# Layer 1 attention: keys and queries turned by 32x32 blocks and through memory instead of on TensorE

## The reference

```python
q = (hidden_states @ Wq + bq).reshape(b, n, H, HD)      # H = 32 heads, HD = 128
k = (hidden_states @ Wk + bk).reshape(b, n, H, HD)
v = (hidden_states @ Wv + bv).reshape(b, n, H, HD)
q = rmsnorm(q, gq)
k = rmsnorm(k, gk)
scores = jnp.einsum('bnhd,bmhd->bhnm', q, k) * scale
attn = jax.nn.softmax(scores.astype(jnp.float32), axis=-1)
out = jnp.einsum('bhnm,bmhd->bnhd', attn, v).reshape(b, n, H * HD)
return out @ Wo + bo
...
x = _layernorm(x + _L1_attn_ref(x, ...), axis=-1)
```

## Time and profile before

| | us |
|---|---|
| median of three runs | 3010.38 (3010.3 to 3012.96) |
| the profiled execution | 3012.17 |
| its span, first to last instruction | 3010.1 |
| layer 1's attention in it | about 1151 to 2737 |
| busy in the span: PE, DVE, ACT, POOL | 2884.7, 2234.3, 1590.2, 1955.5 |

### The profile page before, as it was taken

One profiled execution on the slowest core, in us unless ns is written; L12 is line 12 of the kernel. 1 busy time (PEld: TensorE's weight loads), 2 busy tenths in 40 slices (PEclk: granted clock), 3 DMA queues, 4 the chain that ended last, 5 costly groups with the idle time before them and its releaser, 6 DMA issues. The chain is left out here.

```text
span 3010.1 us, 55474 instructions
## 1 busy us (share of the span) xinstructions
PE 2884.7 (96%) x15712; PEld 2507.0 (83%) x15712; DVE 2234.3 (74%) x3419; ACT 1590.2 (53%) x3145; POOL 1955.5 (65%) x1526
## 2 busy tenths in 40 slices
PE   6999999999999978999999999999999999987998
PEld 5888888888888857889898999989898999975886
DVE  6787887887887856777777777777777777775555
ACT  4444444444444423666666666666666666652221
POOL 7777777777777632666666666666656666655664
PEclk9999999999999999999999999999999999997999
DMA  4334334334334401665666656666665666565551
GB/s 123 116 107 117 107 106 119 104 106 122 101 106 122 123 25 51 197 208 193 205 204 201 204 193 203 197 204 205 196 207 191 204 198 204 194 201 168 151 144 41
DMA packets 310073, 464.10 MB, mean 154 GB/s; under 512 B 30464, under 2 KB 220928, under 8 KB 305792
## 3 DMA queue, kind: packets, MB, share of 16 engines
q1 hardware_dynamic: 272336, 328.37, 37.7%
q10 hardware_dynamic: 37680, 135.02, 11.4%
HBM read 293.41 MB, written 169.87 MB: 154 GB/s over the span
## 5 line engine op out<-in xcount | busy, mean ns | idle before, releaser
L1660 ACT ACTIVATE b_prob<-b_s_ps,b_shift 128x1024 f32<-128x1024 f32 x256 | 286.0, 1117 | 347.4 <-DVE b_shift L1810 340.2
L82 PE MATMUL b_pj_kq<-b_w_hi,xT_hi 128*128 128x384 f32 x1008 | 351.9, 349 | 23.8 <-DVE b_nat L1786 21.4
L83 PE MATMUL b_pj_kq<-b_w_lo,xT_hi 128*128 128x384 f32 x1008 | 342.9, 340 | 0.0
L84 PE MATMUL b_pj_kq<-b_w_hi,xT_lo 128*128 128x384 f32 x1008 | 342.6, 340 | 0.0
L1816 DVE STREAM_TRANSPOSE b_blocks<-b_prob 128x1024 f32<-128x1024 f32 x256 | 317.3, 1239 | 28.4 <-ACT b_prob L1660 27.9
L1567 POOL TENSOR_TENSOR b_rstd<-b_mean_sq,power 128x4 f32<-128x4 f32 x128 | 129.0, 1008 | 320.7 <-DVE b_mean_sq L1796 314.1
L1582 POOL TENSOR_TENSOR b_pT_lo<-b_pT_lo,b_pT_hi 128x1024 fp32r<-128x1024 f32 x128 | 305.0, 2405 | 18.0 <-ACT b_pT_hi L1649 18.0
L1582 POOL TENSOR_TENSOR pT_lo<-pT_lo,pT_hi 128x1024 fp32r<-128x1024 f32 x128 | 305.2, 2407 | 13.2 <-ACT pT_hi L1649 13.2
L1810 DVE TENSOR_REDUCE b_shift<-b_s_ps 128x1 f32<-128x1024 f32 x256 | 306.9, 1199 | 2.8 <-PE b_s_ps L84 2.8
L82 PEld LDWEIGHTS b_pj_kq<-b_w_hi,xT_hi 128*128 128x128 f32 x1008 | 190.4, 189 | 60.8 <-DVE b_nat L1786 45.1
L1341 POOL TENSOR_TENSOR b_w_lo<-b_w_raw,b_w_hi 128x512 fp32r<-128x512 f32 x96 | 124.4, 1297 | 152.0 <-ACT b_w_hi L1334 134.5
(11 more groups left out here) (345 smaller groups left out, 9383.5 us busy)
## 6 DMA issues: line engine op xcount, KB each, us to landing
bounce<-b_blocks ACTq DMA_DIRECT2D x256, 512.0 KB, 3.5
pT_lo<-bounce SPq DMA_DIRECT2D x512, 128.0 KB, 3.1
b_pT_lo<-bounce SPq DMA_DIRECT2D x512, 128.0 KB, 2.8
kv_bounce<-a_kv_blocks SPq DMA_DIRECT2D x128, 256.0 KB, 4.3
a_kv_raw<-kv_bounce SPq DMA_DIRECT2D x32, 1024.0 KB, 4.8
b_w_raw<-in_w SPq DMA_DIRECT2D x32, 768.0 KB, 4.9
b_w_raw<-in_w SPq DMA_DIRECT2D x95, 256.0 KB, 3.2
a_w_raw<-in_w SPq DMA_DIRECT2D x32, 256.0 KB, 3.1
```

The source lines that it names most:

```text
L82: pe.matmul(out, w_hi, x_hi, start=first, stop=False, skip_group_check=partial)
L83: pe.matmul(out, w_hi, x_lo, start=False, stop=False, skip_group_check=partial)
L84: return pe.matmul(out, w_lo, x_hi, start=False, stop=last, skip_group_check=partial)
L1660: act.activation(prob[t % 2][:, :], s_ps[t % 2][:, :], ACT.Exp, bias=shift[:, t:t + 1], accum_out=row_sum[:, t:t + 1]).then_inc(exp_done, 1)
```

## The change

Keys and queries are no longer transposed by TensorE.

- VectorE turns the scaled keys and queries of two tiles by 32x32 blocks, one instruction for the keys and one for the queries (`turn_kq`, 128x256 each), in the odd slot, ahead of `take`. ScalarE's queue writes the result to `kq_bounce` in memory (`write_kq`, 256 KB, rows of 2 KB), right behind `kq_high`. SyncE reads it back with four DMAs of 64 KB in pieces of 512 bytes (`move_kq`) into `kq_raw`, ahead of the four that read a tile's probabilities. Bounce and `kq_raw` have two buffers each.
- `kq_high` reads `kq_raw` in SBUF instead of a PSUM bank and stands first in the odd slot, ahead of `v_high` and `write_blocks`. `kq_low` reads `kq_raw` too, stands ahead of `transpose_blocks`, and has three instructions instead of two (keys 128x256, queries 128x128 twice).
- To make room for the way through memory, the preparation of a batch (squares to turning) comes two slots earlier, and the projection too: `prepared` and `projected` replace the old offsets. v's splits move to slots 1 and 5 (two batches) and 7, the weight splits to slots 0, 1 and 2. `nat` of the first batch has two buffers.
- SyncE's `step` now begins with tiles 4 to 7 of the last head and ends with tile 3 of its own; the load of the weights moves with the start of the step.
- The half bank of the transposes becomes a second output bank: odd tiles of `output_tile` go to `y_odd`, so the wait is for the addition before last.
- Some semaphores are merged; `inverse_rms` waits for `kq_scaled` instead of `exp_done`.

```diff
-        nat = [sb(f"nat{i}", [P, BATCH, KQV]) for i in range(NB)]
+        nat_first = [sb(f"nat0{b}", [P, BATCH, KQV]) for b in range(2)]
+        nat_rest = [sb(f"nat{i}", [P, BATCH, KQV]) for i in range(1, NB)]
+        kq_blocks = [sb(f"kq_blocks{i}", [P, GROUPS, 2, BATCH, BLK]) for i in range(2)]
+        kq_bounce = [nc.dram_tensor(f"kq_bounce{i}", (GROUPS, BLK, GROUPS, 2 * BATCH * BLK), F32) for i in range(2)]
+        kq_raw = [sb(f"kq_raw{i}", [P, GROUPS, 2, BATCH, BLK]) for i in range(2)]
...
-        pj, kq_ps = pj_kq[:, 0:HALF], pj_kq[:, HALF:].rearrange("p (k n) -> p k n", k=2)
+        pj, y_odd = pj_y[:, 0:HALF], pj_y[:, HALF:]
...
-            if s < 6:
-                return (h + 1, 1 - b, s + 2) if nxt else None
-            return (h + 2, b, s - 6) if more else None
+            if s < 4:
+                return (h + 1, 1 - b, s + 4) if nxt else None
+            return (h + 2, b, s - 4) if more else None
+
+        def prepared(h, b, nxt, more, s):
+
+            i = s // 2 + 1
+            if i < NB:
+                return (h + 1, 1 - b, i) if nxt else None
+            return (h + 2, b, 0) if more else None
...
-        SPLITS = {1: 0, 2: 1, 4: 2}
+        def v_batches(h, b, cur, nxt, s):
+
+            if s == 1:
+                return ((h, b, 3),) if cur else ()
+            which = {5: (0, 1), 7: (2,)}.get(s, ())
+            return [(h + 1, 1 - b, i) for i in which] if nxt else ()
+
+        SPLITS = {0: 0, 1: 1, 2: 2}
...
+            def move_kq(g, i):
+
+                sp.wait_ge(kq_written, 16 * (NB * g + i + 1))
+                sp.sem_inc(room, 1)
+                wait(sp, kq_lo_done, NB * g + i - 1)
+                for c in range(GROUPS):
+                    sp.dma_start(kq_raw[i % 2][c * BLK:(c + 1) * BLK].rearrange("y r k u x -> y r (k u x)"),
+                                 kq_bounce[i % 2][:, :, c, :].rearrange("r y n -> y r n")).then_inc(kq_moved, 16)
...
-                if rest:
-                    move(h - 1, NT - 1)
-                for t in range(NT - 1):
+                for t in range(NT // 2, NT):
+                    if t == 4 and cur:
+                        move_kq(h, 3)
+                    if t == 6 and nxt:
+                        move_kq(h + 1, 0)
+                    if rest:
+                        move(h - 1, t)
+                for t in range(NT // 2):
+                    if t % 2 == 0 and nxt:
+                        move_kq(h + 1, t // 2 + 1)
                     if cur:
                         move(h, t)
...
-                act.wait_ge(kq_tr, NB * g + i + 1)
+                act.wait_ge(kq_moved, 16 * GROUPS * (NB * g + i + 1))
                 wait(act, scored, NT * (g - 1))
-                act.activation(k_hi[bg][:, cut], kq_ps[:, 0, :], ACT.Copy)
-                act.activation(q_hi[bg][:, cut], kq_ps[:, 1, :], ACT.Copy, scale=gain[:, 0:1]).then_inc(kq_hi_done, 1)
+                act.activation(in_blocks(k_hi[bg][:, cut]), from_blocks(i, 0), ACT.Copy)
+                act.activation(in_blocks(q_hi[bg][:, cut]), from_blocks(i, 1), ACT.Copy,
+                               scale=gain[:, 0:1]).then_inc(kq_hi_done, 1)
+
+            def write_kq(g, i):
+
+                act.wait_ge(kq_blocked, 2 * (NB * g + i + 1))
+                wait(act, kq_written, 16 * (NB * g + i))
+                wait(act, kq_moved, 16 * GROUPS * (NB * g + i - 1))
+                act.dma_start(kq_bounce[i % 2][:, :, :, :].rearrange("r y c n -> (r y) (c n)"),
+                              kq_blocks[i % 2][:, :, :, :, :].rearrange("p c k u x -> p (c k u x)")).then_inc(
+                    kq_written, 16)
...
-                wait(pe, y_added, NT * h + (t - 1 if peeled(h, HEADS - 1) and t >= 3 else t))
+                wait(pe, y_added, NT * h + t - 1)
...
-                    if nxt and s % 2:
-                        transpose_kq(h + 1, s // 2)
...
                 dve.wait_ge(kq_hi_done, NB * g + i + 1)
-                dve.tensor_tensor(k_lo[bg][:, cut], kq_ps[:, 0, :], f(k_hi[bg][:, cut]), ALU.subtract)
-                dve.scalar_tensor_tensor(out=q_lo[bg][:, cut], in0=kq_ps[:, 1, :], scalar=gain[:, 0:1],
-                                         in1=f(q_hi[bg][:, cut]), op0=ALU.mult,
-                                         op1=ALU.subtract).then_inc(kq_lo_done, 1)
+                dve.tensor_tensor(in_blocks(k_lo[bg][:, cut]), from_blocks(i, 0), f(in_blocks(k_hi[bg][:, cut])),
+                                  ALU.subtract)
+                for u in range(BATCH):
+                    one = slice(i * WIDE + u * P, i * WIDE + (u + 1) * P)
+                    last = dve.scalar_tensor_tensor(
+                        out=q_lo[bg][:, one].rearrange("p (r x) -> p r x", r=GROUPS), in0=kq_raw[i % 2][:, :, 1, u, :],
+                        scalar=gain[:, 0:1], in1=f(q_hi[bg][:, one]).rearrange("p (r x) -> p r x", r=GROUPS),
+                        op0=ALU.mult, op1=ALU.subtract)
+                last.then_inc(kq_lo_done, 1)
+
+            def turn_kq(g, bg, i):
+
+                dve.wait_ge(kq_scaled, NB * g + i + 1)
+                wait(dve, kq_written, 16 * (NB * g + i - 1))
+                for k in range(2):
+                    dve.transpose(kq_blocks[i % 2][:, :, k, :, :].rearrange("p c u x -> p u c x"),
+                                  nat_of(bg, i)[:, :, k * HD:(k + 1) * HD].rearrange(
+                                      "p u (c y) -> p u c y", c=GROUPS)).then_inc(kq_blocked, 1)
...
                 for s in range(NT):
                     q = quarter(h, b, cur, rest, s)
-                    if nxt and s % 2 == 0:
-                        means(h + 1, s // 2)
+                    ready = prepared(h, b, nxt, more, s)
+                    if s % 2 == 0 and ready:
+                        means(ready[0], ready[2])
+                    if s % 2 and ready:
+                        turn_kq(*ready)
                     if projected(h, b, nxt, more, s):
                         take(*projected(h, b, nxt, more, s))
+                    if nxt and s % 2:
+                        kq_low(h + 1, 1 - b, s // 2)
...
-                    if nxt and s % 2:
-                        kq_low(h + 1, 1 - b, s // 2)
```

More of the change, by code:

```diff
@@ L1443, in y_bank, with nat_of @@
         def y_bank(h, t):
-            return pj if peeled(h, HEADS - 1) and t >= 3 and t % 2 else y_ps[:, :]
+            return y_odd if t % 2 else y_ps[:, :]
+        def nat_of(bg, i):
+            return nat_rest[i - 1] if i else nat_first[bg]
         def project_bank(g, t):
@@ L1585, in step @@
                 for s in range(NT):
-                    if nxt and s % 2 == 0:
-                        inverse_rms(h + 1, 1 - b, s // 2)
-                    if v_batch(h, b, cur, nxt, s):
-                        v_low(*v_batch(h, b, cur, nxt, s))
+                    if s % 2 == 0 and prepared(h, b, nxt, more, s):
+                        inverse_rms(*prepared(h, b, nxt, more, s))
+                    for which in v_batches(h, b, cur, nxt, s):
+                        v_low(*which)
                     if split_batch(h, cur, rest, s):
@@ L1682, in step @@
                         write_blocks(h, s - 1)
-                    if nxt and s % 2:
-                        kq_high(h + 1, 1 - b, s // 2)
                     if cur:
@@ L1711, in project_tile @@
                 last.then_inc(proj, 1)
-            def transpose_kq(g, i):
-                pe.wait_ge(kq_scaled, NB * g + i + 1)
-                wait(pe, kq_lo_done, NB * g + i)
-                for kind in range(2):
-                    for u in range(BATCH):
-                        last = pe.transpose(kq_ps[:, kind, u * P:(u + 1) * P], nat[i][:, u, kind * HD:(kind + 1) * HD],
-                                            sh.ident[:, :])
-                last.then_inc(kq_tr, 1)
             def values(h, b, i, part):
@@ L1783, in take @@
                 if u == 0:
-                    wait(dve, kq_tr, NB * (g - 1) + i + 1)
-                    wait(dve, v_lo_done, NB * (g - 1) + i + 1)
-                dve.tensor_tensor(nat[i][:, u, :], project_bank(g, t), bias_sb[bg][:, :], ALU.add).then_inc(taken, 1)
+                    before = NB * (g - 1 if i else g - 2) + i + 1
+                    wait(dve, kq_blocked, 2 * before)
+                    wait(dve, v_lo_done, before)
+                dve.tensor_tensor(nat_of(bg, i)[:, u, :], project_bank(g, t), bias_sb[bg][:, :], ALU.add).then_inc(taken, 1)
                 if peeled(g, 0) and t == 1:
```

71 lines of the change are left out of this document (36 added, 35 removed).

## The result

The changed kernel takes 3187.33 us (median of four runs, 3186.48 to 3193.05) where the kernel before takes 3011.32. The ratio is 1.0587, with a 95% interval of 1.0573 to 1.0600: slower by 176 us, against 158 forecast.

What follows compares the result with a forecast made beforehand. The prediction took the ScalarE-VectorE loop, as long as the head, as the bound. Terms 142 (29 heads), 4 (steps 0 and 30) and 12 (start) sum to +158 on 3010.38, giving 3168 us; own range 3120 to 3215, 8-in-10 range 3018 to 3230.

Steps and rivals of the forecast that it cites:

- 142 + 4: Head loop: 29 full heads at 4.9 us more each make 142; steps 0 and 30 together add 4.
- The loop between ScalarE and VectorE has the length of the head: Layer 1: the gapless chain from exponential to exponential makes 47.84 of a head's 48.04 us; TensorE sits just under it.
- Two SBUF inputs exclude GpSimd: Odd slots: VectorE's two-SBUF-input low parts and GpSimd's SBUF-reading instructions exclude each other for their whole length; forecast chance 0.72.
- rival 1: Odd slots: VectorE and GpSimd don't exclude each other here; head 46.6 us, time 2979 us; chance 0.11.
- rival 2: Odd slots: only the plain form is held, not the queries' fused form; head as before, 3022 us; chance 0.07.
- The odd slots: Slots 1, 3, 5, 7: low parts alternating with GpSimd's instructions give 28.3 us together against 23.2 before, +5.1.
- Even slots 24.64: Even slots have no low parts with two SBUF inputs, so they keep their 24.64 us a head.
- the 3 us of slack for landings: Turned keys and queries land at E + 10.3 us, needed by kq_high at E + 13 or later; E starts the even exponential.
- Start +12: Start of the stage: four batches' trips through memory, uncovered, +9 us, and head 1's first batch +4; taken as +12, 6-18.
- Rival 3: Held and something more: lower TensorE clock (sign: under 1.00 mid stage) or late memory way holding kq_high; 3285 us; chance 0.08.
- The DMA share: Each head moves 4 x 512 KB more, so the DMA share goes from 0.62 to about 0.76; not a bound.
- Rival 4: TensorE alone is the bound: 2.3 us a head less, 66 in all, with +12 at the start 2956; chance 0.02.

Runs made afterwards that it cites:

- experiment 5: Changed kernel with 64 satisfied waits (32 instructions) ahead of ScalarE's head loop, which moves from 688-975 to 720-1007: 3142.93 us, ratio 1.0432.
- experiment 9: Changed kernel with low parts' second input from PSUM (wrong numbers) and ScalarE's loop moved by 32 satisfied-wait instructions: 3041.61 us, ratio 1.0107.
- experiment 2: Changed kernel with kq_low moved on VectorE to the end of the odd slot, behind the output's addition: 2974.31 us, ratio 0.9861.
- experiments 1 and 4: 1: changed kernel, low parts' second input from PSUM, 3085.44 us; 4: kernel before, low parts with both inputs in SBUF, 3048.76 us; both compute wrong numbers.
- experiment 10: Changed kernel with ScalarE's loop moved and only the keys' low part taking its second input from PSUM; queries' fused form keeps two SBUF inputs: 3102.80 us.
- experiment 6: Changed kernel with kq_low at the odd slot's end and 64 satisfied waits (32 instructions) ahead of ScalarE's loop: 2953.28 us, ratio 0.9804.

## Why the prediction came out right

By experiments 5 and 9 the 176 us are, in medians: 30 without either cause (3041.6 - 3011.3), **101 for the exclusion of the two engines** (3142.9 - 3041.6), **44 for fetching instructions** (3187.3 - 3142.9). The forecast had the mechanism of the larger part and the sign. That its sum is so near is luck: for what it describes, the kernel with the loop moved, it gave 158 where 132 were measured, and the 44 that it did not see stood against these 26 too many. Most of the 26 is in the heads: 142 + 4 forecast, (51.47 - 47.74) x 31 = 116 measured.

- *The loop between ScalarE and VectorE has the length of the head.* Right. TensorE lost its transposes and gained nothing. When the low parts left that loop (experiment 2), the time fell.
- *Two SBUF inputs exclude GpSimd* (rival 1 false). Shown by experiments 1 and 4. *The fused form too* (rival 2 false): experiment 10. The Trainium skill's rule ("SBUF — State Buffer", Who interferes with whom) held for the form that no row had shown.
- *The odd slots.* Forecast 7.7, 7.05, 7.1 and 6.45 us for slots 1, 3, 5 and 7, 28.3 in all. With the loop moved they measure 7.30, 6.83, 6.66 and 6.25 in one head, 27.04. In the slot shown above E is 1921.33, and the keys' part ends where forecast (E + 2.81 against 2.84). What follows was sized too long: two value splits and two query parts took 1.5 us behind the keys', not 1.75, and from the turning to the next exponential it was 2.36 (1925.64 to 1928.00), not 2.50. The mean of the keys' part was forecast near 0.9 and is 0.73: in slots 1 and 3 it starts so late, behind the weight copy, that little of GpSimd's row is left. The forecast also has a slip of 0.2 us a head, 6 us in all: its odd slots are 5.1 longer, its head only 4.9.
- *Even slots 24.64.* 24.88 with the loop moved. Once every two heads the one at the loop's top lasted 9.71 on average instead of 6.03. **This is the missing term:** (9.71 - 6.03) x 13 = 48 us, less the 4.1 that the moved kernel loses ahead of the loop, against 44 measured. No step of the forecast counts a loop's instructions; its term for the rest of the loop was zero.
- *The head:* 52.9 forecast for a head in mid stage. There it is 51.9 without the fetches and 53.9 with them (over all heads 51.47 and 53.12).
- *What the exclusion costs against none.* The forecast's first rival put the loop without it at 46.6 us, so the exclusion at 6.3; measured 48.40 and 3.07. The wrong term is the 3 us of slack for landings: without it, slots 1, 3 and 5 are within 0.1 of its 5.75, 5.75 and 5.25, but slot 7 is 6.54 and not 5.25, with ScalarE waiting for the turned keys, and the even slots are 25.2 and not 24.64. So without it this order would still have been slower than before (experiment 9), and not 2979.
- *Start +12:* the first copy +9.1, in the moved kernel +13.2, of which the one wait ahead of its loop is 4.1. *Weight splits 0.2 to 0.3 us longer:* 0.10.
- *Rival 3:* its sign, a clock under 1.00 in mid stage, did show: 0.96 from 1300 to 2600 us. From 1250 to 2800 TensorE waits 170 us for VectorE's additions. In the slot at the loop's top, shown above, the clock falls only after TensorE has stood idle, so there it follows the loss and is not its origin; with the loop moved it is 0.98, with the low parts in PSUM as well (experiment 9) or late (experiment 2) 1.00. No run separates what the lower clock costs by itself; the slot behind the one at the top is only 0.2 us longer than the same slot in experiment 5 (7.5 against 7.3). The DMA share rose to 0.69 and not to 0.76, which was reckoned for a head of the old length. The DMA was on time: ScalarE waited 0.8 us in all for the turned keys.
- *Rival 4 (2956, TensorE alone)* was wrong for this kernel. It is, to 3 us, the time of the version of experiment 6, where TensorE is the bound.

## What to carry to other kernels

When a VectorE instruction in a loop between engines gets a second SBUF input, ask where GpSimd is at that moment. If that instruction arrives in the last piece of a row of GpSimd's work anyway, cutting the row in pieces does not help, and moving the VectorE instruction behind it does. Here one moved call turned +176 us into -37, and 32 idle instructions ahead of a loop took off another 21.
Count the instructions of each engine's loop, waits included, before and after a change, and look at the packets of the instruction queue: a jump there is a cost that no edit shows.

## What the runs showed of the hardware that was not expected

A loop of 287 instructions on ScalarE shows no wait on "issue" at 720 to 1007 and loses about 2 us twice a pass at 688 to 975, in two different kernels; one of 271 at 676 to 947 loses only the first of the two; one of 246 at 656 to 902 none. Packets of the instruction queue: 29 to 32 without the waits, 95 or 96 with them. The second wait stands before instruction 696 in both kernels, though that is `pT_hi` in the one and `o_hi` in the other.

What follows is inferred and was not tried by itself: that ScalarE's store holds two pieces of the program, too few to keep the first one of a loop of three. A border just ahead of 696 and a second one between 902 and 947, with the third behind 1007, would fit all these runs.

The Trainium skill ("Advanced Engine Details and Errata", ISA Cache) gives two lines of 16 KB, 256 instructions each. The runs agree with it only in part: 256 behind 696 is 952, which the loop at 688 to 975 crosses and the one at 656 to 902 does not; but the one at 676 to 947 ends just short of it and still has the first wait and 96 packets, and no run here shows why.
